# Graph streams by tiles of 128 edges, with one sum for each tile, in place of slots of two tiles

## What is computed

```python
e = leaky(es[src] + ed[dst])
m = segment_max(e, dst, n)
ex = exp(e - m[dst])
s = segment_sum(ex, dst, n)
alpha = ex / s[dst]
out = segment_sum(alpha[:, :, None] * z[src], dst, n)
```

## Time and profile before

| | us |
|---|---|
| median of three runs | 5789.2 |
| the profiled execution | 5784.15 |
| its span, first to last instruction | 5782.4 |
| TensorE busy (PE) | 4086.9 (71%) |
| VectorE busy (DVE) | 3472.9 (60%) |
| GpSimd busy (POOL) | 3350.9 (58%) |
| ScalarE busy (ACT) | 2748.9 (48%) |
| gathers L992 in layers 1 and 2, 1856 of them | 1800.2 busy, 675.5 idle before them |
| adds L1106, 1392 of them | 588.1 busy, 163.6 idle before them |

### The profile page before, as it was taken

The page is one execution under the profiler, slowest core; times in us unless marked ns, Lnnn a source line. Parts: engine busy times, 40 slices in busy tenths (PEclk is TensorE's granted clock), DMA queues, the critical chain, the costliest instruction groups (busy, mean ns, idle before and its releaser), DMA issues.

```text
span 5782.4 us, 74758 instructions
## 1 busy us (share of the span) xinstructions
PE 4086.9 (71%) x17795; PEld 2853.5 (49%) x17795; DVE 3472.9 (60%) x10666; ACT 2748.9 (48%) x5933; POOL 3350.9 (58%) x3492
## 2 busy tenths in 40 slices
PE   1997666766662697868777776655656565797998
PEld 1655554544542585556655555534444444333665
DVE  4367766666677536867888887755555555722111
ACT  0455766666661233578888887522222222243222
POOL 0113777777765744377777777377777777211222
PEclk9998777787785698978988998878777877898999
DMA  3194555555542344244544445344444444210110
GB/s 99 59 261 123 145 139 141 139 139 139 139 111 70 113 123 119 80 132 131 133 132 132 132 132 137 95 132 129 128 129 129 128 128 129 71 43 27 37 32 27
DMA packets 347488, 660.26 MB, mean 114 GB/s; under 512 B 78834, under 2 KB 196608, under 8 KB 346664
## 3 DMA queue, kind: packets, MB, share of 16 engines
q0 software_dynamic: 156336, 433.90, 28.0%
q1 hardware_dynamic: 190732, 221.57, 13.2%
HBM read 541.11 MB, written 115.45 MB: 114 GB/s over the span
## 4 chain that ended last, share of the span: by engine, by line
PE 24%; issue 14%; DVE 12%; POOL 12%; DMA 4%; ACT 3%; DVEq 1%; POOLq 0%; SPq 0%; ACTq 0%
POOL AR L992 8%; PE ps L1216 6%; PE ps L2592 3%; PE ps L2573 3%; DMA AR<-D_z,SRCI 3%; PE ps L2281 3%; PE ps L2069 2%; POOL AR L1670 2%; DVE AR L1106 2%; PE ps L2293 1%; POOL D_sx L1660 1%; DVE AR L1079 1%; DVE AR L1084 1%; PE ps L1178 1%; PE ps L2058 1%
## 5 line engine op out<-in xcount | busy, mean ns | idle before, releaser
L992 POOL DMA_INDIRECT AR<-D_z,SRCI x1856 | 1800.2, 970 | 675.5 <-issue 502.1
L1216 PE MATMUL ps<-AR 128*128 128x264 f32 (+2 forms) x5568 | 1784.1, 475 | 209.9 <-DVE AR L1079 72.4
L1216 PEld LDWEIGHTS ps<-AR 128*128 128x128 f32 x5568 | 1254.3, 236 | 525.0 <-issue 152.7
L992 POOL DMA_INDIRECT AR<-D_h,SRCI x904 | 871.8, 964 | 277.3 <-issue 244.6
L1106 DVE TENSOR_TENSOR AR<-ps,AR 128x264 f32 (+2 forms) x1392 | 588.1, 423 | 163.6 <-DVE AR L1106 128.8
L1263 ACT ACTIVATE AR<-iota_n,NREL 128x128 f32<-128x128 f32 x1856 | 587.2, 389 | 13.2 <-PE ps L1216 10.2
L1084 DVE TENSOR_TENSOR AR<-AR,ps 128x1024 f32<-128x1024 f32 x464 | 558.3, 1203 | 0.0
L1186 PE MATMUL ps<-ident,AR 128*128 128x128 f32 (+2 forms) x174 | 60.2, 346 | 648.5 <-DVE AR L1027 648.5
L1025 DVE TENSOR_TENSOR AR<-AR 128x128 f32<-128x128 f32 (+2 forms) x174 | 49.1, 282 | 781.6 <-SPq L969 779.8
L1280 ACT ACTIVATE AR<-ps 128x128 f32<-128x128 f32 (+2 forms) x174 | 46.5, 267 | 832.4 <-PE ps L1186 827.3
L1276 ACT ACTIVATE AR<-AR,ones 128x1024 bf16<-128x1024 bf16 x348 | 399.5, 1148 | 11.3
(11 more groups left out here) (442 smaller groups left out, 7755.0 us busy)
## 6 DMA issues: line engine op xcount, KB each, us to landing
AR<-D_rel SPq DMA_DIRECT2D x348, 256.0 KB
D_sx<-AR SPq DMA_DIRECT2D x8, 6370.0 KB
AR<-D_z,SRCI POOLq DMA_INDIRECT x1856
AR<-D_h,SRCI POOLq DMA_INDIRECT x928
D_y<-AR SPq DMA_DIRECT2D x106, 128.0 KB, 1.7
AR<-in_L_ffn_Wd SPq DMA_DIRECT2D x8, 1024.0 KB, 12.0
AR<-D_mask SPq DMA_DIRECT2D x58, 128.0 KB
D_h<-AR SPq DMA_DIRECT2D x49, 132.0 KB, 1.7
```

The source lines that it names most:

```text
L992: e.indirect_dma_start(out=GV[:, u % 48, :], out_offset=None, in_=D_row[L.i], in_offset=bass.IndirectOffsetOnAxis(ap=SRCI[:, u:u + 1], axi ...
L1216: t = e.matmul(banks[n % 3][:, 0:YW], Sr[:, u % 8, :], GV[:, u % 48, L.GW - YW:L.GW], start=(i == 0), stop=(i == 1))
```

## The change

The tile is 128 edges instead of 256. NT becomes 832, and with 48 crossings of blocks there are NU = 880 units, which are themselves the slots; before there were 928 units in 464 slots. A stream has 55 groups of 16 units instead of 58. Each unit is gathered once and has a sum of its own: quad issues each product with start and stop, and add runs once for each unit, so 16 times in a group instead of 8. The ring of sum banks has four banks instead of three. In layers 0 and 2 it takes bank 3; in layer 1, where bank 3 is the side work's, it takes bank 7, and the weights have bank 6 alone, so back() waits there until the last weigh of the group before is done. expand steps its register for each unit. The preparation has seven rounds of 128 slots of 128 edges instead of four of 128 slots of 256 edges, and 37 words of steps instead of 20.

The core of the diff (in the preparation, buffers and loops over j change in the same way as the few lines shown):

```diff
-NT = 416
-NS = NT + 48
-NSP = 512
-NU = 2 * NS
+NT = 832
+NU = NT + 48
+NSP = 896
+NJ = NSP // 128
 NG2 = NU // 16
-NW = 20
+NW = 37
...
-        self.s0 = NS * i
+        self.s0 = NU * i
...
             e.wait_ge(gf_ps, 1)
-            e.tensor_copy(gb[:, :], banks[0][:, 0:NT]).then_inc(*dv.up())
-            for j in range(4):
+            e.tensor_copy(gb[:, 0:512], banks[0][:, 0:512])
+            e.tensor_copy(gb[:, 512:NT], banks[1][:, 0:NT - 512]).then_inc(*dv.up())
+            for j in range(NJ):
...
-                u = slice(256 * j, 256 * j + 256)
-                e.tensor_copy(NREL[:, u].rearrange("p (s v) -> p v s", v=2), banks[2][:, 0:256].rearrange("p (v s) -> p v s", v=2))
-                e.tensor_copy(SRCI[:, u].rearrange("p (s v) -> p v s", v=2), banks[2][:, 256:512].rearrange("p (v s) -> p v s", v=2)).then_inc(cols_copied, 1)
-            e.wait_ge(keys_in, 64)
-            before, here, behind = kw[:, :, 0:256], kw[:, :, 1:257], kw[:, :, 2:258]
-            SA, SB = same[:, 0:1024], same[:, 1024:2048]
-            e.tensor_tensor(SA.rearrange("p (j l) -> p j l", j=4), here, before, ALU.is_equal).then_inc(*dv.up())
-            e.tensor_tensor(SB.rearrange("p (j l) -> p j l", j=4), here, behind, ALU.is_equal).then_inc(*dv.up())
+                u = slice(128 * j, 128 * j + 128)
+                e.tensor_copy(NREL[:, u], banks[2][:, 0:128])
+                e.tensor_copy(SRCI[:, u], banks[2][:, 128:256]).then_inc(cols_copied, 1)
...
-        BK_AD, BK_T, BK_W = banks[4], banks[5], banks[6:8]
+        BK_AD, BK_T = banks[4], banks[5]
+        BK_W = (banks[6:8], [banks[6], banks[6]], banks[6:8])
+        BK_S = (banks[0:4], banks[0:3] + [banks[7]], banks[0:4])
...
                 if u >= 48 and u % 2 == 0:
-                    e.wait_ge(slot_mm, L.s0 + (u - 48) // 2 + 1)
+                    e.wait_ge(slot_mm, L.s0 + u - 48 + 2)
...
-                w = BK_W[K % 2][:, 4 * H * q:4 * H * q + 4 * H].unsqueeze(2).to_broadcast([128, 4 * H, D])
+                w = BK_W[L.i][K % 2][:, 4 * H * q:4 * H * q + 4 * H].unsqueeze(2).to_broadcast([128, 4 * H, D])
                 e.tensor_tensor(G, G, w, ALU.mult).then_inc(m_ready, 1)
...
-                at = walk.to(8 * g, YW, WORDS)
+                at = walk.to(16 * g, YW, WORDS)
...
-                if s % 8 == 0:
-                    e.wait_ge(scaled, L.k0 + s // 8 + 1)
+                if s % 16 == 0:
+                    e.wait_ge(scaled, L.k0 + s // 16 + 1)
                 else:
                     e.wait_ge(slot_added, n)
-                e.tensor_tensor(o, banks[n % 3][:, 0:YW], o, ALU.add).then_inc(slot_added, 1)
+                e.tensor_tensor(o, BK_S[L.i][n % 4][:, 0:YW], o, ALU.add).then_inc(slot_added, 1)
...
-                        add(8 * g - 2, None)
-                        add(8 * g - 1, None)
+                        for u in range(16 * g - 4, 16 * g):
+                            add(u, None)
...
-                    add(8 * g, at)
-                    add(8 * g + 1, None)
+                    add(16 * g, at)
+                    for u in range(16 * g + 1, 16 * g + 4):
+                        add(u, None)
                 side.before_carry(e, k)
                 if more:
                     carry(k)
                 if g >= 0:
                     weigh(g, 2)
-                    add(8 * g + 2, None)
-                    add(8 * g + 3, None)
+                    for u in range(16 * g + 4, 16 * g + 8):
+                        add(u, None)
                 side.before_reference(e, k)
                 if more:
                     reference(k)
@@ -1152,11 +1156,11 @@
                     weigh(g, 3)
                 side.after_weigh3(e, k)
                 if g >= 0:
-                    add(8 * g + 4, None)
-                    add(8 * g + 5, None)
-            add(NS - 2, None)
-            add(NS - 1, None)
-            e.wait_ge(slot_added, L.s0 + NS)
+                    for u in range(16 * g + 8, 16 * g + 12):
+                        add(u, None)
+            for u in range(NU - 4, NU):
...
-                for s in range(8 * k + 4 * v, 8 * k + 4 * v + 4):
-                    at = bass.ds(walk.to(s, L.TS, WORDS), 3 * H)
-                    for i in range(2):
-                        u = 2 * (s - 8 * k) + i
-                        t = e.matmul(BK_AD[:, 3 * H * u:3 * H * u + 3 * H], OHr[v][:, 128 * (u % 8):128 * (u % 8) + 128], AD3[:, at], start=True, stop=True)
+                for u in range(8 * v, 8 * v + 8):
+                    at = bass.ds(walk.to(16 * k + u, L.TS, WORDS), 3 * H)
+                    t = e.matmul(BK_AD[:, 3 * H * u:3 * H * u + 3 * H], OHr[v][:, 128 * (u % 8):128 * (u % 8) + 128], AD3[:, at], start=True, stop=True)
                 t.then_inc(ad_ps, 1)
...
+                if L.i == 1 and k:
+                    e.wait_ge(m_ready, 4 * (L.k0 + k))
+                w = BK_W[L.i][(L.k0 + k) % 2]
                 e.transpose(w[:, 0:P], B2[0:P, :], ident[0:P, 0:P])
...
-                for s in range(8 * g + 2 * q, 8 * g + 2 * q + 2):
-                    n = L.s0 + s
-                    if n >= 3:
-                        e.wait_ge(slot_added, n - 2)
-                    for i in range(2):
-                        u = 2 * s + i
-                        t = e.matmul(banks[n % 3][:, 0:YW], Sr[:, u % 8, :], GV[:, u % 48, L.GW - YW:L.GW], start=(i == 0), stop=(i == 1))
-                    t.then_inc(slot_mm, 1)
+                for u in range(16 * g + 4 * q, 16 * g + 4 * q + 4):
+                    n = L.s0 + u
+                    if n >= 4:
+                        e.wait_ge(slot_added, n - 3)
+                    e.matmul(BK_S[L.i][n % 4][:, 0:YW], Sr[:, u % 8, :], GV[:, u % 48, L.GW - YW:L.GW], start=True, stop=True).then_inc(slot_mm, 1)
...
-                    e.wait_ge(slot_mm, 2 * Q - 2)
+                    e.wait_ge(slot_mm, 4 * Q - 4)
```

120 lines of the change are left out of this document (63 added, 57 removed).

## The result

The changed kernel takes 6148.7 us (median of 4 runs, 6147.33 to 6149.98), the kernel before 5788.7 on the same chip (5780.65 to 5792.94): ratio 1.0624, 95% interval 1.0608 to 1.0640. It is slower, as forecast, but by 360 us and not by 72. The profiled execution has a span of 6147.7 us, 365.3 more than before.

What follows compares the result with a forecast made beforehand. GpSimd's gather was taken to bound all three layers, with VectorE nearly full in layer 1. Preparation +14, layer 0 -20, layer 1 +132 and layer 2 -54 gave +72 on 5784: 5856 us, whole range 5775 to 5925.

Steps and rivals of the forecast that it cites:

- Gather's period, layer 2: Layer 2: GpSimd's gather stays the bound at 20.7 us a group; three fewer groups save 62, net -54 us.
- Price of an added add: VectorE's chained adds of unit sums: 0.62 us for each added one, eight more a group, 5.0 us a group.
- Rival 3: Chained adds cost only their unchained 0.34 us, so the gather's saving wins: -95 us, 5689 us; chance 9%.
- Preparation: VectorE's chain from slot count to masks gets longer, with nothing beside it to hide it: +14 us (10 to 20).
- TensorE comes later too: Layer 1: eight more register steps in expand put 1.6 to 1.9 us ahead of back() and of L2069.
- I keep 0.9 of the 2.2: Layer 1: of VectorE's 2.2 us of waits a group 0.9 remain, making the period 24.4 us and the layer +132.
- Two engines at the same period disturb each other a little; I take 20.7: Layer 0: VectorE at 20.4 us a group against the gather's 20.3 gives a period of 20.7, -20 us.
- back()'s new wait for weigh 3: Layer 1, one weights bank: weigh 3 is done before TensorE's 16 steps, so costed at nothing; uncovered, below 0.8 us a group.
- Rival 1: VectorE's add chain and TensorE's quads hold each other up through the sum banks: +214 us, 5998 us; chance 10%.
- all 2.2 kept: Layer 1's upper bound: all of VectorE's 2.2 us of waits a group remain, period 25.7 us, +197 us.

Runs made afterwards that it cites:

- c2: Changed kernel with expand(k+1, 0), half of expand, issued before cols on TensorE, all work kept: 5847.2 us, ratio 1.0098 to the kernel before.
- c1: Changed kernel with expand's register stepped only before every second product, leaving out the odd units' right row: 5848.4 us, ratio 1.0099 to the kernel before.
- c6: Kernel before with a second register step, by zero, for each slot in expand, 16 a group, nothing else changed: 5986.0 us, ratio 1.0337.

## Why the prediction was wrong

**Gather's period, layer 2: right.** -58 between the first and the last rescale was forecast; they give -51.3. GpSimd stays the bound there, at 20.80 us against 20.7.

**Price of an added add: right.** 0.62 us was taken. In layer 1 of the changed kernel:

```profile
3205.69 0.42 DVE L1109 TENSOR_TENSOR AR<-ps,AR 128x260 f32 x1
3206.31 0.43 DVE L1109 TENSOR_TENSOR AR<-ps,AR 128x260 f32 x1 [0.21 <-DVE AR L1109]
3207.15 0.43 DVE L1109 TENSOR_TENSOR AR<-ps,AR 128x260 f32 x1 [0.41 <-PE ps L1218]
3207.79 0.43 DVE L1109 TENSOR_TENSOR AR<-ps,AR 128x260 f32 x1 [0.21 <-DVE AR L1109]
```

0.62 to 0.64 apart but for a late sum. With c2, where VectorE hardly waits, the own times are 20.6 and 23.5 for the forecast's 20.4 and 23.5. Rival 3 is out. The Trainium skill ("VectorE: DVE Perf Modes", The DRAIN you can't avoid) says of a chain of copies that the semaphore costs nothing extra; for these adds the rows disagree (0.62 to 0.64 us with it, 0.34 for the two reads of the earlier trace rows without).

**Preparation: the mechanism right, the size short.** +21 in place of +14. Counting was as said; each round of columns takes 2.5 us for the forecast's 2.4, and the first round starts 14.6 us later than before (68.55 against 53.96) where I had some 11.

VectorE's timeline of the changed kernel, first two rounds of columns:

```profile
68.55 0.21 DVE L338 CAST AR<-AR 128x128 f32<-128x128 int32 x1
...
71.02 0.42 DVE L338 CAST AR<-AR 128x128 f32<-128x128 int32 x1
```

**The step that failed: "TensorE comes later too", its size and what I made of it.** The size first. "the 16 products of L1178 took 2941.82 to 2943.74, 1.9 us for 8 steps" misreads: the steps began at 2941.1, under L2058, and three were done by 2941.82. A step is 0.33 us, so "8 more put 1.6 to 1.9 us ahead of back() and of L2069" should have said 2.7. And one group isn't the layer: expand to back() was 1.15 us on average in layer 1 and 0.88 in layer 0, since quad 2 hid most steps. It is 3.81 and 4.09 now, 2.7 and 3.2 us more.

Then the overlap. The longest wait at L2012 "would shrink to 0.7; that for L2069 stays about as it is. I keep 0.9 of the 2.2": measured 4.1 us a group in layer 1. "Two engines at the same period disturb each other a little; I take 20.7": measured 22.67 in layer 0, 1.63 of it the wait of scores for L1180, for which the forecast had 0.3. I set VectorE's delay against TensorE's as if they ran side by side. They lie on one loop, carry to cols to quad 2 to expand to scores (in layer 1 on to L2070). There VectorE's own part between carry and scores grew by four chained adds, 2.6 us, and TensorE's answer in layer 0 by 4.5: 3.2 for the steps, 0.9 for a quad 2 at a lower clock and 0.4 ahead of it. c1 and c2 take eight steps off this way and land at 5848 and 5847 us, 8 and 9 below the forecast of 5856: nearly the whole miss goes with this one term. On the kernel before, c6 has the steps alone cost 195 us.

**back()'s new wait for weigh 3: not seen.** No row of TensorE's waits in layer 1 names it, as forecast.

**Rival 1** came nearest to the total (5998, still 151 short) and is nearer in both layers (21.9 for 22.67, 26 for 27.2), but not in cause: its handshakes are the banks, and these are the same in c2. What it has in common with the truth is a loop between the two engines.

My upper ends, 22 for layer 0 and 197 for layer 1, took "all 2.2 kept" as the worst. A wait has no such ceiling where the engine that it waits for gets longer: with the 2.7 us of steps added in full to the forecast, 53 x 2.7 = 143 us in layer 0 and 49.5 x 2.7 = 134 in layer 1, the upper end would have been about 6133; even that is below the 6149 measured.

## What to carry to other kernels

Ask of each lengthened piece not how long it is but on which loop over two engines it lies; sum the loop on both sides, and take the longer. A piece that the slack of a bound engine hid (the gather here) is not hidden any more once the same change raises another engine to that bound. Short register work of a sequencer can be moved to where its engine idles anyway, at no cost in instructions, but it has to be weighed in each place against who stands behind it.

## What the runs showed of the hardware

A register step of expand is 0.33 us on TensorE's sequencer (16 starts of L96 from 1119.4 to 1124.4), of which the fused instruction is 0.16. Steps can run under products that are already issued: with 8 steps expand to back() took 0.88 us on average in layer 0, with 16 it took 4.09.

A wait of VectorE's add for the one before it puts them 0.62 to 0.64 us apart, and two reads of PSUM without one start 0.34 apart.

The granted clock was 0.88 before, 0.80 in the changed kernel and 0.81 in the kernel before with 16 steps (2700 to 3700 us). Eight passes of L2070 took 3.67 us on average in the changed kernel, against 2.41 before.

On some chips single register instructions are much longer: L96 takes up to 1394 ns there against 183, and before needs 6459 to 6549 us for 5789. The changed kernel loses less on them (1.028 and 1.031 for 1.062), and half of expand earlier is even a little ahead of before. The cause of this was not found.
